# An attention program's hand-written order: fillers moved between steps, one norm split over steps 2, 8 and 9, contexts loaded a sequence sooner

## What is computed

```
x = layernorm(x + mixer_block(x))
x = layernorm(x + cross_attention(x, context, mask))
x = layernorm(x + quantized_mlp(x))
```

```
attn = softmax(q @ k.T + mask);  out = (attn @ v) @ Wout
h = xn @ W1;  val, gate = split(h)
out = out + (silu(gate) * val) @ W2
```

## Time and profile before

| | |
|---|---|
| time before, median of 3 runs | 1804.37 us (1803.83 to 1811.12) |
| the profiled execution | 1809.56 us, span 1807.7 us |
| instructions | 35591 |
| PE matmul busy | 1626.6 us (90%) |
| DVE busy | 1281.2 us (71%) |
| ACT busy | 982.2 us (54%) |
| GpSimd busy | 543.5 us (30%) |
| mean granted TensorE clock | 0.958 of full speed |

### The profile page before, as it was taken

How to read it: one execution, slowest core, us unless ns; L and a number is a source line. 1 busy time by engine, 2 the same in 40 slices (tenths; PEclk the granted TensorE clock), 3 DMA queues, 4 the chain that set the end, 5 groups by cost and what they waited for, 6 DMA issues and landing times.

```text
span 1807.7 us, 35591 instructions
## 1 busy us (share of the span) xinstructions
PE 1626.6 (90%) x13256; PEld 985.6 (55%) x13256; DVE 1281.2 (71%) x3633; ACT 982.2 (54%) x2326; POOL 543.5 (30%) x689
## 2 busy tenths in 40 slices
PE   4479999999999967898998999999999999899897
PEld 2356676676676533454554554455455455455467
DVE  6888989989985566667656657766766666755745
ACT  3444644644532455666655755755665566566552
POOL 3868678678673100200110110110110020011001
PEclk8789999999999978999999999999999999999999
DMA  4000000000012344333333333334334233334210
GB/s 135 11 11 12 21 22 12 31 21 12 21 40 80 102 92 149 88 86 80 79 86 90 73 94 88 79 79 94 82 80 97 65 82 84 83 75 97 57 27 22
DMA packets 177613, 119.24 MB, mean 66 GB/s; under 512 B 113856, under 2 KB 171136, under 8 KB 176544
## 3 DMA queue, kind: packets, MB, share of 16 engines
q1 hardware_dynamic: 176976, 116.50, 25.8%
q10 hardware_dynamic: 464, 0.46, 0.1%
HBM read 96.92 MB, written 7.42 MB: 58 GB/s over the span
## 4 chain that ended last, share of the span: by engine, by line
PE 64%; DVE 21%; issue 4%; DMA 4%; ACT 4%; POOL 3%; DVEq 0%; SPq 0%; POOLq 0%; ACTq 0%
PE ps L1624 15%; PE ps L1615 9%; PE ps L1599 9%; PE ps L1579 7%; PE ps L314 3%; PE ps L387 3%; PE ps L405 3%; DVE m_u L727 3%; PE ps L1684 2%; DVE x_blk L1966 2%; DVE m_rs L759 2%; PE ps L427 2%; DVE x_pr L1952 2%; PE ps L440 2%; DMA x_cx<-in_context 2%
## 5 line engine op out<-in xcount | busy, mean ns | idle before, releaser
L1833 ACT ACTIVATE x_pr<-x_pr,x_rc 128x375 f32<-128x375 f32 x448 | 247.2, 600 | 208.8 <-DVE x_rc L1958 207.7
L1952 DVE CUSTOM_DVE_ANT_0 x_pr<-ps,x_mk 128x375 f32<-128x375 f32 x448 | 226.9, 543 | 187.7 <-PE ps L1579 133.4
L1827 ACT ACTIVATE x_pr<-x_pr,x_mx 128x375 f32<-128x375 f32 x448 | 266.3, 596 | 125.1 <-DVE x_mx L1952 125.1
L1966 DVE STREAM_TRANSPOSE x_blk<-x_pr 128x384 f32<-128x384 f32 x448 | 232.2, 557 | 31.0 <-ACT x_pr L1833 31.0
L1535 POOL TENSOR_TENSOR x_cT<-x_cT,x_rb 128x375 f32<-128x375 f32 x64 | 57.3, 917 | 641.6 <-DMA x_rb<-context_roots 641.6
L1624 PE MATMUL ps<-x_xn,x_w 128*128 128x448 f32 x512 | 221.7, 573 | 21.2 <-DVE x_ff L2017 20.0
L1599 PE MATMUL ps<-x_blk,x_va 32*64 32x224 f32 x6144 | 180.8, 381 | 38.3 <-DVE x_blk L1966 38.3
L1599 PEld LDWEIGHTS ps<-x_blk,x_va 32*64 32x64 f32 x6144 | 149.9, 142 | 82.6 <-issue 78.7
L1579 PE MATMUL ps<-x_kT,x_qT 64*128 64x375 f32 x896 | 183.4, 516 | 9.0 <-ACT x_qT L1854 6.1
L1624 PEld LDWEIGHTS ps<-x_xn,x_w 128*128 128x128 f32 x512 | 98.0, 200 | 122.1 <-issue 87.4
L314 PE MATMUL ps<-m_xa,w_in 128*128 128x448 f32 x352 | 146.7, 564 | 6.2 <-ACT m_xa L532 6.2
(11 more groups left out here) (205 smaller groups left out, 2773.8 us busy)
## 6 DMA issues: line engine op xcount, KB each, us to landing
x_mk<-in_mask SPq DMA_DIRECT2D x224, 187.5 KB, 2.6
x_va<-x_vT SPq DMA_DIRECT2D x256, 48.0 KB, 2.1
x_cx<-in_context SPq DMA_DIRECT2D x32, 375.0 KB
x_cT<-in_context_turned SPq DMA_DIRECT2D x32, 375.0 KB, 3.9
x_rb<-context_roots SPq DMA_DIRECT2D x32, 187.5 KB, 5.3
m_Rd<-bc_roots SPq DMA_DIRECT2D x8, 448.0 KB, 3.5
x_mixed<-m_x SPq DMA_DIRECT2D x8, 448.0 KB, 3.9
X<-x_mixed SPq DMA_DIRECT2D x8, 448.0 KB, 4.3
```

Source lines behind the costliest of these rows:

```text
L1827: act.activation(pr[:, k, 0:J], pr[:, k, 0:J], ACT.Exp, scale=-1.0, bias=mx[:, k:k + 1], accum_out=sums[:, k:k + 1]).then_inc(h_e.sem, 1)
L1833: act.activation(pr[:, k + e, 0:J], pr[:, k + e, 0:J], ACT.Copy, scale=rc[:, k + e:k + e + 1]).then_inc(h_n.sem, 1)
L1952: dve.tensor_tensor_reduce(pr[:, k + e, 0:J], bank(SCORE_BANKS[p % NP] + e)[:, 0:J], mk[:, p % SLOT, :], -1.0, 3.0e38, ALU.add, ALU.min, m ...
L1966: dve.transpose(blocks[:, place_of(p), e, :, :].rearrange("p c x -> p (c x)"), pr[:, 2 * (p % SLOT) + e, :]).then_inc(h_t.sem, 1)
```

## The change

- `FINAL` goes from (27, 1, 2) to (2, 8, 9): statistics in step 2 of group i + 2, roots in step 8, application at step 9; the store moves from step 6 to step 11 of SyncE's list.
- PE executes list X ahead of the scores where r = 2 (steps 2, 9, 16, 23).
- The tables of places change so that steps with r = 1 hold no filler. Query 4 goes from step 1 to step 0; out part 0 from 0 to 2 and the parts after it back by about one; out part 6 from 8 to list X of 9; value 0 from 11 to 12, value 1 from 12 to 13, gate 3 from 15 to 14; up 2 from 22 to 21. Values stand in list X now and gates in list Y, so in every step a value comes ahead of a gate.
- Seats: query 4 from 0 to 1, value 0 from 2 to 3, value 1 from 3 to 0.
- SyncE loads the context of three sequences on at r = 5, behind a wait for the statistics of the one before it, where it loaded the context of two sequences on at r = 2, ahead of the broadcast roots.

Group 0 has its own table for gates and values, and no out, back, up or down; its places are unchanged.

```diff
-FINAL = (STEPS - 1, 1, 2)
+FINAL = (2, 8, 9)
...
     for n, p in enumerate(OUT_AT):
-        at[p, "Y"].append(("out", n // KA, n % KA))
+        at[p, "X" if p == 9 and n == 6 else "Y"].append(("out", n // KA, n % KA))
     for f in range(KH):
-        at[GATE_AT[f], "X"].append(("gate", f))
-        at[VALUE_AT[f], "Y"].append(("value", f))
+        at[VALUE_AT[f], "X"].append(("value", f))
+        at[GATE_AT[f], "Y"].append(("gate", f))
     for n, p in enumerate(UP_AT):
-        at[p, "Y" if p != 25 else "X"].append(("up", n))
+        at[p, "X" if n in (3, 7) else "Y"].append(("up", n))
...
-QUERY_AT = (25, 26, 27, 0, 1, 2, 3, 3)
+QUERY_AT = (25, 26, 27, 0, 0, 2, 3, 3)
...
-SEAT = {"gate": (1,) * 8, "value": (2, 3) + (0,) * 6, "out": (1, 0), "kv": (2,) * 4, "query": (1, 1, 0, 0, 0, 0, 2, 3),
+SEAT = {"gate": (1,) * 8, "value": (3,) + (0,) * 7, "out": (1, 0), "kv": (2,) * 4, "query": (1, 1, 0, 0, 1, 0, 2, 3),
...
+        def next_context(i, b):
+
+            j, c = (i, b - 1) if b else (i - 1, GB - 1)
+            sp.wait_ge(c_ln.sem, c_ln.value(j, CROOT * c + 2 * JT))
+            contexts(i, b)
+
...
-                if p == 6 and it >= 2:
+                if p == 11 and it >= 2:
                     result(it - 2)
...
+                if first and p == 0:
+                    next_context(0, 2)
+                if r == 5 and (it * GB + b + 3) // GB < NG:
+                    next_context(*divmod(it * GB + b + 3, GB))
...
-                    if g + (n + 1) // GB < NG:
-                        contexts(g + (n + 1) // GB, (n + 1) % GB)
...
         def group(it, first=False, last=False):
             for p in range(STEPS):
+                if p % NP == 2:
+                    parts(it, p, "X", first, last)
                 for ahead in SCORED[p % NP] if p or not first else (0,):
...
-                parts(it, p, "X", first, last)
+                if p % NP != 2:
+                    parts(it, p, "X", first, last)
...
-                if not first and not last and p == FINAL[0]:
-                    final_norm(it - 1, 0)
+                if it >= 2 and p == FINAL[0]:
+                    final_norm(it - 2, 0)
```

More of the change, by code:

```diff
@@ L1104, in schedule_first @@
     return first
-OUT_AT = (0, 2, 3, 4, 6, 7, 8, 9, 4, 5, 5, 6, 9, 10, 10, 11)
-GATE_AT, VALUE_AT = (10, 12, 13, 15, 16, 17, 18, 19), (11, 12, 14, 16, 17, 18, 19, 20)
-UP_AT = (20, 21, 22, 23, 23, 24, 24, 25)
-QUERY_AT = (25, 26, 27, 0, 1, 2, 3, 3)
+OUT_AT = (2, 3, 4, 6, 7, 7, 9, 9, 4, 5, 5, 6, 10, 10, 11, 11)
+GATE_AT, VALUE_AT = (10, 12, 13, 14, 16, 17, 18, 19), (12, 13, 14, 16, 17, 18, 19, 20)
+UP_AT = (20, 21, 21, 23, 23, 24, 24, 25)
+W1_AT = 10
+QUERY_AT = (25, 26, 27, 0, 0, 2, 3, 3)
 LAST_READ = (23, 24, 25, 26, 27, 27, 22, 22)
@@ L1542, in final_normed @@
         def final_normed(i):
-            pool.wait_ge(c_ln.sem, c_ln.value(i + 2, CROOT * 2))
+            pool.wait_ge(c_ln.sem, c_ln.value(i + 2, CROOT * 3))
             rooted(pool, 3, lambda b: so[:, b, :], lambda b: so[:, b, :], f_nm)
@@ L2090, in group @@
                         context_roots(it, n, slice(0, 2))
-                    elif n == 1 and it >= 2:
+                    elif n == 2 and it >= 2:
                         dve.wait_ge(f_ln.sem, f_ln.value(it - 2, f_ln.per))
```

## The result

| | before | after |
|---|---|---|
| median of the runs | 1805.75 us (4 runs, 1803.83 to 1811.12) | 1749.72 us (4 runs, 1745.28 to 1752.62) |
| the profiled execution | 1809.56 us, span 1807.7 | 1751.45 us, span 1749.6 |
| mean granted TensorE clock | 0.958 | 0.965 |

The ratio is 0.9683, with a 95% interval of 0.9651 to 0.9714: 56.0 us less. The forecast was 35.5 us less (1768.9), with a range of 1747 to 1789 that holds the result, 3 us inside its lower end.

The account below looks back on a forecast made before the run. PE's work, waits and clock were taken to bound the kernel. The terms 24.9 + 5.3 + 11.6 - 10.9 - 3.3 + 7.9 = 35.5 us, off 1804.4, gave 1768.9 us, range 1747 to 1789.

Parts of the forecast that it names:

- What bounds the kernel: The time is PE's work (busy 90% of the span), its waits (10.0 us a group) and what the clock takes.
- Steps 0 to 2: PE's wait of 2.21 us becomes 0.75, that of 0.87 goes, step 0's clock falls go: 24.9 us gained.
- kv 2 and steps 12 to 17: The 0.76 us wait ahead of kv 2 goes, 5.3 us gained; steps 12 to 17 wait less, 11.6 us gained.
- Steps 18 to 24: Waits of 1.45 us become 3.45 in groups 1 to 6, mostly at token: 10.9 us lost in all.
- Contexts: Sooner loads remove waits in group 0, 7.9 us gained; nothing in groups 1 to 7.
- The clock in the other places: 12 clock falls at steps 17 and 24 in place of 10 at steps 14 and 17: 3.3 us lost.
- most waits of 2.03 us were followed by a fall: Argument, from ftoken's wait in step 17, against all 12 remaining clock falls going.
- The clock stays up: Rival: the waits left don't bring PE's clock down, all 12 falls go, 19.8 us: 1749.1 us; chance 0.2.
- The fillers are paid in full: Rival: fillers ahead of scores in steps 2, 9, 16, 23 add 47.6 us: 1828.1 us; chance of slower 0.05.
- DVE sets the pace: Rival: behind step 14 DVE is late for step 16, gain only 13.7 us: 1790.7 us; chance 0.18.
- GpSimd beside DVE: Rival: GpSimd works beside DVE at step 16 in every group, costing 4.6 us: 1773.5 us; chance 0.05.

Follow-up runs that it names:

- A and C: The changed kernel with value 4 ahead of ftoken in step 17 and the tokens' statistics behind step 20's other DVE work: 1732.39 us, ratio 0.9596.

## Why the prediction was right, and where its size was off

**What bounds the kernel.** Right: PE with its waits and its clock. Take waits away and the time goes down by them, in every run but one: A and C, where the trace got shorter and the median did not.

**Steps 0 to 2.** Right. 0.64 us of wait for 0.75, the 0.87 gone, and no fall behind the product in any group. The norm alone gave 18 us, for 19 in the forecast (6 x (1.46 + 1.7)). With the old norm back the time rises by 13.4 us.

**kv 2 and steps 12 to 17.** Right: 0.76 gone, 1.93 to 0.16, 0.75 gone, 2.03 to 2.58 with a forecast of 2.65. The chain behind gate 4 through ACT's tanh was read correctly. This part is the largest: 31 us alone, of which 17 are waits.

**Steps 18 to 24.** Right in sign and mechanism: the gain of the moved queries and up 2 is lost again at token. Value 7's seat cost 1.03 us and not 1.45.

**Contexts.** 7.4 us of group 0 in the traces for 7.9 forecast, of which 5.4 show in the product's time, as the mixer happened to end 2.0 us later. The waits for loads went, but PE still waits 7.04 us ahead of kv 3, for GpSimd, which starts at 714.51 when the roots' broadcast has landed, hardly another time than the 714.15 of before.

**The clock in the other places: the term that was mis-sized.** I counted 10 falls before at steps 14 and 17 and 12 after, one for each wait of 2.65 us and five in six for those of 2.0: -3.3 us. The price and the count come from the trace of before: the product of step 0 took 4.21 us at a granted clock of 0.59, that of step 7 took 2.53 at 1.00, 1.7 us less, and a mean of 0.97 over 570 us is 17 us of lost clock, nine or ten such falls in four groups. Four of them stand at step 0, and the five or six left over make two in three of the eight waits at steps 14 and 17. The trace does have these 10 in seven groups beside the six of step 0. After has 4 in place of 12: three of seven at ftoken, one of six at token. At 1.65 us each that is 13 of the 20.5 us by which the forecast fell short. The waits, a little shorter than forecast (6.24 for 7.25 us a group), are 7 more, and the contexts take 0.5 off; the 1 us that is left is less than one kernel's runs differ by. The step that failed is "most waits of 2.03 us were followed by a fall": the share of one place in one kernel was carried to another place and another order. The same wait of 2.21 us in step 0 was followed by a fall in six of six groups before, in five of six with new gates and values, and in three of six with only the norm put back.

**The rivals.** *The clock stays up* gave 1749.1, and the median is 1749.7. That is in part a coincidence: four falls were left, and the shorter waits make up for them. But it was nearer to what happened than the forecast, which had it at 0.2. *The fillers are paid in full*: refuted, putting them back changes nothing. *DVE sets the pace*: refuted by the waits, and by a further 32 us with the same work on DVE. *GpSimd beside DVE*: did not happen, the norm took its 404 to 408 ns in all 28 operations. The two no longer overlap in the changed kernel. With gates, values and list X put back together (1784.06 us) they do, and in three groups of seven the norm is longer by it: 2.04 to 2.08 us for its four operations, which take 1.38 in the other four groups. In group 2 GpSimd's first instruction has started when DVE comes to the fourth operation of the norm:

```profile
976.82 1.16 POOL L1544 TENSOR_TENSOR x_cT<-x_cT,x_rb 128x375 f32<-128x375 f32 x1 [33.44 <-DMA x_rb<-context_roots]
977.07 1.07 DVE L1375 TENSOR_SCALAR x_so<-x_so,x_mv,x_rt 112x256 f32<-112x256 f32 x1
```

DVE's operation takes 1.07 us where the others take 0.41, and ends 0.16 us behind GpSimd's. The one before it had started first, at 976.74; it took its 0.41 us, and GpSimd's instruction 1.16 us, for the 0.98 of group 5 (1399.97), where the norm was over by then. So where two met here it was the one that started second that became longer, on either engine. Why it did, no run shows. The 0.65 us of the earlier trace rows are of the same kind: one operation of the four took 1.07 us, beside a first instruction of GpSimd of 1.11. So the rival's price was right, 0.66 to 0.71 us at ftoken (2.69 to 2.74 us for 2.03).

## What to carry to other kernels

Where one engine sets the pace in a repeating period, list every wait of one period with what ended it, and cost each edit in that list; here nine such entries were each within 0.5 us. Price the clock apart from the waits and with a wide margin: a wait near 2 us may cost 1.7 us more or nothing, and the share of waits that do can't be carried from one order to the next. What worked here is to bring every wait well under that (none of up to 1.1 us was followed by a fall), by putting one more piece of work ahead of the piece that waits; three such moves gave another 32 us.

## What the runs showed of the hardware

In groups 1 to 7 of all fourteen traces I set each wait of PE of 0.6 us or more beside the stretches of low granted clock that begin around its end:

| wait of PE | how many | with a fall |
|---|---|---|
| 0.6 to 1.1 us | 227 | 0 |
| 1.4 to 1.99 us | 65 | 10 |
| 2.0 to 2.3 us | 46 | 29 |
| 2.4 to 2.8 us | 67 | 41 |

No wait of up to 1.1 us was followed by a fall. Between 1.8 and 2.6 us waits of equal length to 0.01 us, at the same place of the order, were or were not. The order ahead of them, in the trace of one kernel, was the same, and no experiment here isolates what decides between them: that stays open. The last line holds four waits of 2.69 to 2.74 us, which are ftoken's 2.03 us lengthened by GpSimd's instruction as above. A fall costs 1.7 us where PE has work all through it (2.53 to 4.21, 3.19 to 4.88).

The clock is also a large part of what makes runs of one kernel differ, by 4 to 16 us: of nine runs of the kernel before, the shortest took 1797.85 us at a mean clock of 0.963, the longest 1813.79 at 0.950. It is not all of it: two runs of the kernel with the new final norm alone took 1781.15 and 1788.94 us, both at 0.965. The mixer, the same code in all fourteen traces, ends between 610.2 and 618.2 us (the first kv piece). Parts worth less than that are better read in the stretch that they change than in the whole time.
